# Second attention of a four-block transformer kernel: the order of TensorE's work inside one unit

## What is computed

```python
def _L1_xattn_ref(x, context, Wq, bq, Wk, bk, Wv, bv, Wo, bo):
    q = (x @ Wq.T + bq).reshape(B, N, 16, 16).transpose(0, 2, 1, 3)
    k = (context @ Wk.T + bk).reshape(B, M, 16, 16).transpose(0, 2, 1, 3)
    v = (context @ Wv.T + bv).reshape(B, M, 16, 16).transpose(0, 2, 1, 3)
    attn = softmax(einsum('bhnd,bhmd->bhnm', q, k) * 16 ** -0.5)
    out = einsum('bhnm,bhmd->bhnd', attn, v)
    return out.transpose(0, 2, 1, 3).reshape(B, N, C) @ Wo.T + bo
x = x + tanh(g_xattn[1]) * _L1_xattn_ref(layernorm(x), ctx_1024, ...)
```

## Time and profile before

| | |
|---|---|
| time, median of 3 runs | 3599.64 us (3598.19 to 3603.85) |
| the profiled execution: its time, its span | 3601.34 us, 3599.3 us |
| first attention | about 170 to 2425 us of the span |
| second attention, first to last scores | 2741.8 to 3444 us |
| busy over the whole span | PE 86%, DVE 68%, POOL 58%, ACT 48% |
| the same from 2741.5 to 3448 us (706.5 us) | PE 581.5 us, DVE 483.8 us, ACT 485.8 us, POOL 110.9 us |
| a projection's matmuls to its first lay DMA (unit 4, step 3) | 2927.31 to 2931.45 us: ACT's copy 0.69, POOL's two parts 0.61 and 1.16 us |
| a DMA of `a_q_op<-a_hi`, issue to landing | 1.8 us, median of 128 |

### The profile page before, as it was taken

How to read it: one execution, slowest core, us unless ns; L and a number is a source line. 1 busy time by engine, 2 the same in 40 slices (tenths; PEclk the granted TensorE clock), 3 DMA queues, 4 the chain that set the end, 5 groups by cost and what they waited for, 6 DMA issues and landing times. The chain is left out here.

```text
span 3599.3 us, 53337 instructions
## 1 busy us (share of the span) xinstructions
PE 3112.9 (86%) x21716; PEld 1181.8 (33%) x21716; DVE 2459.2 (68%) x2971; ACT 1725.8 (48%) x1811; POOL 2094.9 (58%) x985
## 2 busy tenths in 40 slices
PE   3599999999999999999999999985836888888747
PEld 1233433433333333333333343323511222222214
DVE  5567677766777677677667767826546777777648
ACT  3144444444444444444444445443313667766633
POOL 0087897798788788888888788892013121211022
PEclk7699999999999999999999999996957999999969
DMA  1000000000000000000000000001011000000000
GB/s 56 0 5 1 1 7 1 1 7 1 1 7 1 1 1 7 1 1 7 1 1 2 1 1 1 1 1 44 1 29 53 4 19 4 14 4 8 1 0 24
DMA packets 29283, 28.98 MB, mean 8 GB/s; under 512 B 9517, under 2 KB 26606, under 8 KB 29038
## 3 DMA queue, kind: packets, MB, share of 16 engines
q1 hardware_dynamic: 29038, 25.57, 2.4%
HBM read 17.68 MB, written 2.10 MB: 5 GB/s over the span
## 5 line engine op out<-in xcount | busy, mean ns | idle before, releaser
L410 POOL TENSOR_TENSOR a_acc_p<-a_acc_p,a_prob 128x1024 f32<-128x1024 f32 x704 | 1717.4, 2440 | 356.1 <-ACT a_prob L468 284.2
L468 ACT ACTIVATE a_prob<-slot,a_mask_bias 128x1024 f32<-128x1024 f32 x928 | 989.8, 1111 | 926.3 <-PE slot L685 923.4
L502 DVE TENSOR_REDUCE a_part_max<-wide 128x2 f32<-128x1024 f32 x896 | 1091.1, 1218 | 496.6 <-PE wide L666 488.4
L700 PE MATMUL bank<-a_prob,a_val 128*64 128x512 f32 x3712 | 895.5, 604 | 0.2 <-ACT a_prob L468 0.2
L1070 ACT ACTIVATE a_prob<-slot,a_mask_bias 128x1024 f32<-128x1024 f32 x416 | 443.3, 1113 | 189.7 <-PE slot L1256 187.4
L1120 DVE TENSOR_REDUCE a_part_max<-wide 128x1 f32<-128x512 f32 x514 | 336.6, 684 | 137.8 <-PE wide L1244 86.6
L666 PE MATMUL wide<-a_k_hi,a_q_hi 64*128 64x512 f16 (+1 forms) x2048 | 360.3, 364 | 63.2 <-DVE a_part_max L502 58.4
L700 PEld LDWEIGHTS bank<-a_prob,a_val 128*64 128x64 f32 x3712 | 226.3, 136 | 435.0 <-issue 320.6
L685 PE MATMUL slot<-a_q_hi,a_k_hi 64*128 64x512 f16 x1856 | 353.1, 377 | 9.0 <-DVE a_k_lo L493 4.8
L685 PE MATMUL slot<-a_q_lo,a_k_hi 64*128 64x512 f16 x1856 | 352.6, 377 | 0.0
L685 PE MATMUL slot<-a_q_hi,a_k_lo 64*128 64x512 f16 x1856 | 352.5, 376 | 0.0
(11 more groups left out here) (295 smaller groups left out, 3224.6 us busy)
## 6 DMA issues: line engine op xcount, KB each, us to landing
a_w_staged<-in_w SPq DMA_DIRECT2D x8, 384.0 KB, 3.2
x_res<-in_x SPq DMA_DIRECT2D x1, 2048.0 KB, 9.1
a_q_op<-a_hi SPq DMA_DIRECT2D x128, 16.0 KB, 1.8
out_x<-x_res SPq DMA_DIRECT2D x16, 128.0 KB, 1.7
nx_context<-in_ctxt SPq DMA_DIRECT2D x1, 1601.0 KB, 6.6
a_w_staged<-in_w1a SPq DMA_DIRECT2D x4, 385.0 KB, 3.5
ctx_rows<-in_ctx SPq DMA_DIRECT2D x1, 1536.0 KB
a_k_op<-a_hi SPq DMA_DIRECT2D x96, 16.0 KB, 1.8
```

What stands on the lines that cost most here:

```text
L410: nc.gpsimd.tensor_tensor(acc, before, prob[:, k % R, :], ALU.add).then_inc(added_p, 1)
L468: nc.scalar.activation(prob[:, k % R, :], slot[:, :], ACT.Exp, bias=mbias[:, t:t + 1]).then_inc(probs_ready, 1)
L502: nc.vector.reduce_max(part_max[:, w % 2, :, j, c], pairs, AX.X).then_inc(max_used, 1)
L700: ins = nc.tensor.matmul(av[r, :], val[g % 2][:, t, r], prob[:, k % R, h * QB:(h + 1) * QB], start=(t == 0), stop=(t == NT - 1), tile_posi ...
```

## The change

PE's instructions are the same, in another order. In every step the task comes ahead of the scores. Value matmuls of one key tile `n` come at step 2n+5, tile 0 at step 7 together with tile 1; tiles 11 and 12 of a unit fall on steps 1 and 3 of the next. All other work of PE but the second projection, which shares step 11 with a key tile, stands on steps without value matmuls: projections at 2, 11, 16 (before 3, 7, 11), `den` 8 (6), `spread` 10 (9), `outputs` 14 and 18 (15, 19). `turn` stays at 22. ACT's copy moves from step 2 to 4. ACT, DVE, POOL and SP follow the same constants, so their reads, their maxima and their DMA issues are moved with them.

```diff
-        self.job_at = (3, 7, 11)
-        self.raw_at, self.den_at, self.spread_at, self.out_at = 2, 6, 9, (15, 19)
+        self.job_at = (2, 11, 16)
+        self.raw_at, self.den_at, self.spread_at, self.out_at = 4, 8, 10, (14, 18)
         self.neg_at, self.turn_at = 20, 22
+        at = [7] + [2 * n + 5 for n in range(1, self.nt)]
+        self.values_at = [[] for _ in range(self.steps)]
+        for n, s in enumerate(at):
+            self.values_at[s % self.steps].append((s // self.steps, n))
...
                 for s in range(S):
-                    scores(w, s)
                     n = w * S + s + a.lead
                     if n < a.units * a.tasks:
                         task(n)
-                    if s % 4 == 1:
-                        if s > 1:
-                            for t in (s // 2 - 2, s // 2 - 1):
-                                values(w, t)
-                        elif w:
-                            values(w - 1, NT - 1)
+                    scores(w, s)
+                    for ago, n in a.values_at[s]:
+                        if w >= ago:
+                            values(w - ago, n)
                     if job_of(w, s) is not None:
                         project(job_of(w, s))
...
-            values(last, NT - 1)
+            for s in range(S):
+                for ago, n in a.values_at[s]:
+                    if ago:
+                        values(last, n)
             den(last)
```

More of the change, by code:

```diff
@@ L1258, in scores, with values @@
                 ins.then_inc(scores_ready, 1)
-            def values(w, t):
+            def values(w, n):
                 g, u = divmod(w, NU)
-                k = w * S + 2 * t
-                if t == 0:
+                k = w * S + 2 * n
+                if n == 0:
                     if u == 0:
@@ L1270, in values @@
                     r = slice(h * a.pitch, (h + 1) * a.pitch)
-                    ins = nc.tensor.matmul(av[r, :], val[g][:, t, r], prob[:, (k + h // 2) % R, h % 2 * QB:(h % 2 + 1) * QB],
-                                           start=(t == 0), stop=(t == NT - 1), tile_position=(0, h * a.pitch))
+                    ins = nc.tensor.matmul(av[r, :], val[g][:, n, r], prob[:, (k + h // 2) % R, h % 2 * QB:(h % 2 + 1) * QB],
+                                           start=(n == 0), stop=(n == NT - 1), tile_position=(0, h * a.pitch))
                 ins.then_inc(av_done, 1)
```

## The result

| | before | changed |
|---|---|---|
| time, median | 3601.47 us (4 runs, 3598.19 to 3603.85) | 3542.13 us (4 runs, 3538.58 to 3544.19) |
| ratio | 1 | 0.9835, 95% interval 0.9818 to 0.9852 |
| profiled execution: time, span | 3601.34, 3599.3 us | 3543.01, 3541.1 us |

What follows compares the result with a forecast made beforehand. No engine was full; waits among PE, DVE and ACT bound second attention. Gains of 30 us (units 1 to 11), 2 (unit 0), 13 (12 to 14) and 5 (15), less 1 for SP, made 49: 3550.6 us, range 3538 to 3585.

Steps and rivals of the forecast that it cites:

- T to T: Second attention: time between task starts on PE in successive steps; 1.54 us with one key tile, 1.18 after it.
- The sum of a unit: Steps 0 to 25 of second attention added up: 41.5 us against 43.35 before, ahead of clock falls.
- The edges between kinds of matmul: Around PE's value blocks: each splitting costs 0.14 us, five more blocks a unit 0.7 us, held within the 1.00.
- The rival: Tiling changes around value blocks cost more in the new order: 3571 expected, 3612 at the far end; chance 0.08.
- a splitting: Pair of key tiles, 1.86 us, made into two single blocks of 1.00 each: 0.14 us more PE time.
- SP: SP's queue: third projection's lays delay the next unit's shift, 0.2 us net in six units, 1 us in all.
- The clock: TensorE's clock in second attention: a fall in every second unit, 0.7 us a unit, making 42.2.
- Units 12 to 14: Units of second attention without the three projections: 39.3 us twice and 37.5 against 129.0 before, 13 us gained.
- units 0 to 11: Second attention: 30 us gained in units 1 to 11, 2 in unit 0, less 1 for SP.
- The rest of the span: Everything outside the second attention stage: nothing touched, gain 0.
- The slower rival: TensorE's clock falls several times a unit, value blocks at 1.2 GHz: 8 us a unit, 3679; chance 0.05.

Runs made afterwards that it cites:

- x12_two_fixes_filled: Changed kernel with the shift ahead of the third lay, projections at 2, 12, 16, and scores matmuls of steps 4 to 6 issued three times: 3522.3 us, 0.9772.

## Why the prediction was right

- **T to T as the measure, and its terms.** Predicted 1.54 and 1.18 us for a step with and without a key tile, 1.77 for `den`, `spread` and `turn`, 2.40 for the pair, 2.94 for step 11; the trace has 1.54, 1.18, 1.78, 2.39 and 2.94. The sum of a unit was 41.5 us; without a late shift and with a full clock it measured 41.14, or 41.0 in the mean of units 1 to 11, since other projections are a little shorter. The difference to 41.14 is step 20, which takes 1.00 and not 1.18, since its task is one of the two short ones of 65 columns, and an output at 18 with the step behind it, 3.04 and not 3.17.
- **The edges between kinds of matmul.** The rival had 0.32 us a block as its far end. Scores to values 0.31 us, values to the next task 1.00: nothing beyond what was counted. By the rule of the Trainium skill, TensorEngine Tiling (Array Packing), section Key Properties, a change of mode drains the engine; the 0.14 us that a splitting costs may be that drain, and no run here shows more of it.
- **SP.** The place and the mechanism were right, the size was not. I had the shift's issues 1.5 us late, the scores 0.9 and the net at 0.2 us in six units, 1 us in all. In unit 4, 24 lay issues took 16.6 us (0.69 each, 2934.11 to 2950.69), the shift's issues came 2.6 us late (at 2950.80, where 0.29 us behind the cast's start of 2947.93 is 2948.22), and the scores were 1.92 us late (2952.55 to 2954.47). The task ahead covers 0.74 of that (the scores may start 0.96 us behind it and not 0.22 before they hold up the next task at 1.18), and what goes beyond counts in full: 1.17 us there (2953.51 to 2954.68 for the next task). The lateness is the term that was off: the 24 issues took 0.6 us longer than at my 0.67 each, and `turn` came 0.4 us earlier behind the first of them, and since 0.74 us are free, 1.0 us more of waiting is 1.0 us more of cost. Freeing the queue gave 10 us, of which two clock falls fewer are some 3. The term was 1 us and should have been about 7, of which 1 is a fall of the clock behind the late shift in unit 1.
- **The clock.** I took a fall in every second unit at 1.33 us; the profiled run had a low clock at the start of unit 0, three falls at step 7 (units 4, 6, 9) at 1.6 to 1.7 us each (4.03 to 4.09 us T to T, not 2.39), and the one at step 1 of unit 1 that is counted under SP. The three are 5 us where I had 10 for units 1 to 14. Units 12 to 14 had no fall, where I had 0.7 us each; that is a half of the 4 us that they gained beyond the forecast. Without a fall a unit there took 38.22 us (unit 13), not 38.6.
- **Luck.** That units 0 to 11 came out at 32.5 us, where I had 31, comes of errors that nearly cancel. The late shifts and unit 0 cost 7 us more than I had (unit 0 took 45.69 us, longer than the 44.73 before, where I had it 2 us shorter than the mean of 44.96); the units were 0.5 us shorter than my 41.5, 5.6 us in eleven, and the falls in them 2.8 us less.
- **The rest of the span** gave 3.8 us that the forecast did not have; 2.1 of them are the start of the first scores, which scatters as much among the other versions.
- The slower rival, clock falls everywhere, had its deciding point at 2.7 us a unit (the forecast gain of 49 us over 16 units is 3.1, so this was worked out too low); the stage's clock went up, to 0.98.

## What to carry to other kernels

Measure the distance between the same instruction of two steps for each kind of step, and lay a new order out with these lengths; it gave a unit to 1% here. Work hides only in the steps whose length another engine sets, so spreading the long blocks and moving the other work out of their way belong together: 15 and 5 us alone, 51 together, of which some 20 are the clock. When a step moves, follow its DMAs through the issuing queue up to the next transfer behind them; and look for stretches in which PE only waits, since the price of a fallen clock is paid by the block behind them.

## What was not expected

- Work that does nothing made three kernels faster: 192 matmuls in waiting time gave 9, 15 and 9 us (the first 9 hold 2.6 that the filling did not give). What they bought is TensorE at its upper level in the block behind.
- The same work did not always meet the same clock: in one profiled execution each, the same stretch of steps 4 to 6 was followed by three falls in one kernel, one in the next and five in a third, which differ by microseconds elsewhere. What decides it, no run shows. The four runs of the kernel without such a stretch lie within 1.0 us (3508.32 to 3509.34), those of the changed kernel within 5.6; but the runs of `x12_two_fixes_filled`, whose profiled execution had no fall at all, lie within 4.9, so falls are not the only source of scatter.
